# Two embedding tables move from gathers to one-hot products in the last batch, and the blocks between a tile's Gram chunks are set in another order

## The reference

```python
e = jnp.stack([tbl_0[ids[:, 0]], ..., tbl_25[ids[:, 25]]], axis=1)
combined = jnp.concatenate([e, r_dense_x[:, None, :]], axis=1)
interact = jnp.einsum('bfd,bgd->bfg', combined, combined)
z = interact[:, _TRIU_I, _TRIU_J]
h = jnp.concatenate([z.reshape(z.shape[0], -1), r_dense_x], axis=1)
h = jnp.maximum(h @ W_top1 + b_top1, 0.0)
h = jnp.maximum(h @ W_top2 + b_top2, 0.0)
y = h @ W_top3
```

## Time and profile before

| | |
|---|---|
| median of 3 runs | 385.13 us (384.95 to 386.6) |
| the profiled execution | 386.03 us, of which its span is 384.2 us |
| PE busy | 334.0 us, 87% |
| DVE, ACT, POOL busy | 61%, 49%, 70% |
| mean granted PE clock | 0.969 |

### The profile page before, as it was taken

One profiled execution on the slowest core, in us unless ns is written; L12 is line 12 of the kernel. 1 busy time (PEld: TensorE's weight loads), 2 busy tenths in 40 slices (PEclk: granted clock), 3 DMA queues, 4 the chain that ended last, 5 costly groups with the idle time before them and its releaser, 6 DMA issues.

```text
span 384.2 us, 12018 instructions
## 1 busy us (share of the span) xinstructions
PE 334.0 (87%) x5327; PEld 242.1 (63%) x5327; DVE 233.0 (61%) x389; ACT 186.9 (49%) x281; POOL 270.8 (70%) x288
## 2 busy tenths in 40 slices
PE   4999599778688989888998999988997899899776
PEld 3677477566576656557676666557676454578665
DVE  6889799687885829276896929467793011303030
ACT  6587634544515345345444434356444454655323
POOL 7777777777777777777777777777777777777100
PEclk9999989989989999989999999999999999989699
DMA  7998233433332423413343332423212221222000
GB/s 188 255 256 232 77 89 90 99 77 86 82 89 76 86 74 82 111 51 90 77 106 86 85 80 62 119 66 85 78 54 52 56 57 50 57 57 53 19 4 2
DMA packets 24195, 33.61 MB, mean 87 GB/s; under 512 B 6527, under 2 KB 17538, under 8 KB 24144
## 3 DMA queue, kind: packets, MB, share of 16 engines
q0 software_dynamic: 8960, 18.37, 18.2%
q1 hardware_dynamic: 15184, 14.48, 16.1%
HBM read 32.82 MB, written 0.01 MB: 85 GB/s over the span
## 4 chain that ended last, share of the span: by engine, by line
PE 54%; POOL 19%; issue 11%; DVE 7%; ACT 4%; DMA 3%; POOLq 0%; SPq 0%; DVEq 0%; ACTq 0%
POOL gat L372 19%; PE prod L431 12%; PE prod L433 11%; PE gram L460 8%; PE back L502 6%; PE front L405 5%; PE back L506 4%; DVE ring L708 4%; PE back L492 2%; ACT ct L600 1%; DVE ring L702 1%; DMA oh_last<-in_tbl,idx 1%; DMA gat<-in_tbl 1%; PE prod L417 1%; PE back L487 1%
## 5 line engine op out<-in xcount | busy, mean ns | idle before, releaser
L372 POOL DMA_INDIRECT gat<-in_tbl,idx x272 | 260.8, 959 | 83.0 <-issue 81.8
L708 DVE TENSOR_SCALAR ring<-idb,rowid 125x516 fp32r<-125x516 int32 x216 | 145.9, 741 | 16.9 <-PE prod L433 16.6
L431 PE MATMUL prod<-ring,tab_hi 125*128 125x512 f32 x264 | 110.0, 417 | 6.9 <-DVE ring L708 3.8
L433 PE MATMUL prod<-ring,tab_lo 125*128 125x512 f32 x264 | 106.1, 402 | 0.0
L600 ACT COPY ct<-front 128x512 f32<-128x512 f32 (+2 forms) x80 | 72.7, 964 | 25.0 <-PE front L405 22.6
L715 DVE COPY z<-gram 128x216 f32<-128x216 f32 x32 | 12.2, 382 | 111.1 <-PE gram L460 111.1
L460 PE MATMUL gram<-ct 128*32 128x27 f32 x4096 | 56.1, 196 | 17.1 <-issue 9.9
L460 PEld LDWEIGHTS gram<-ct 128*32 128x32 f32 x4096 | 46.7, 109 | 34.1 <-issue 24.8
L431 PEld LDWEIGHTS prod<-ring,tab_hi 125*128 125x128 f32 x264 | 51.4, 195 | 22.8 <-issue 8.4
L433 PEld LDWEIGHTS prod<-ring,tab_lo 125*128 125x128 f32 x264 | 51.2, 194 | 10.2
L405 PE MATMUL front<-ident,gat 128*128 128x128 f32 x272 | 42.7, 283 | 9.7 <-ACT ct L600 3.8
(11 more groups left out here) (73 smaller groups left out, 226.8 us busy)
## 6 DMA issues: line engine op xcount, KB each, us to landing
idb<-in_ids_t SPq DMA_DIRECT2D x27, 258.0 KB, 4.1
gat<-in_tbl,idx POOLq DMA_INDIRECT x272
oh<-in_tbl SPq DMA_DIRECT2D x3, 448.0 KB
oh<-in_dense_t SPq DMA_DIRECT2D x4, 256.0 KB, 3.1
gat<-in_tbl SPq DMA_DIRECT2D x2, 448.0 KB
h<-in_tbl SPq DMA_DIRECT2D x2, 448.0 KB
w1z<-in_w SPq DMA_DIRECT2D x1, 702.0 KB
w2s<-in_w SPq DMA_DIRECT2D x1, 512.0 KB
```

Source lines behind the costliest of these rows:

```text
L372: nc.gpsimd.indirect_dma_start(out=gat[:, t % GS, i, :], out_offset=None, in_=tables[GATHERED[i]][:, :], in_offset=bass.IndirectOffsetOnAx ...
L431: nc.tensor.matmul(prod[:, :], tab_hi[0:OH_P, m, k, :], ring[0:OH_P, k, 0:SB], start=(k == 0), stop=False)
L433: nc.tensor.matmul(prod[:, :], tab_lo[0:OH_P, m, k, :], ring[0:OH_P, k, 0:SB], start=False, stop=(k == OH_K - 1)).then_inc(used, 1)
L708: nc.vector.tensor_scalar(ring[0:OH_P, k, :], idb[0:OH_P, n % IDB, :, 0:IW], rowid[0:OH_P, k:k + 1], None, ALU.is_equal).then_inc(built, 1)
```

## The change

- Tables 7 and 10 (`LATE`, 1250 rows) are put last among the gathered columns. In tiles 12 to 15 they are not gathered: a tile has 15 gathered columns and four fills there. Their rows for the last batch are made by one-hot products in tile 12 (step `X`, ten chunks of 125 rows, 20 matmuls for a table). For this SP loads both tables to the unused half of `oh` late in batch 2, ACT splits off the high parts (step `V`, tile 11) and copies the rows to Gram banks (step `W`, tile 12), DVE subtracts for the low parts and builds the chunks, ACT copies the products (`copy_late_products`) and places them for each tile (step `Q`).
- In batches 0 to 2 a layer block or a one-hot field now stands between Gram chunks 1 and 2 of every tile; `H` is half a field.
- The first batch's extra gathers come with the first fill, not the last.
- In tile 15 and the tail the layer blocks and the pairs' transposes are put in another order, the second layer's matmuls go input by input, and the last two results are stored with one DMA.

```diff
+LATE = [7, 10]
+GATHERED = [f for f in range(26) if f not in ONEHOT + LATE] + LATE
+def fills_of(t):
+    return TF if t < LATE_T else (NG - NL + TCH - 1) // TCH
...
-        return T[0:1] + N[4:5] + T[1:2] + N[5:6] + T[2:3] + Z + T[3:4] + N[6:7] + E[0:4] + T[4:5] + G + E[4:7]
+        return T[0:1] + N[4:5] + T[1:2] + N[5:6] + Z + T[2:3] + N[6:7] + E[0:3] + T[3:] + E[3:4] + G + E[4:5]
     if last and u == 0:
-        return T[0:2] + J[0:0] + T[2:4] + Z + T[4:5] + J[0:2] + G[0:1] + PL + G[1:2] + J[2:3] + G[2:4]
+        return (X[0][0:1] + T[0:2] + X[0][1:] + T[2:3] + X[1][0:1] + Z + T[3:] + J[0:1] + X[1][1:] + [("Q", t)] + J[1:2]
+                + G[0:1] + PL + G[1:2] + J[2:3] + G[2:4])
...
     if u == 0:
-        return T[0:2] + O[0:1] + T[2:3] + Z + T[3:4] + J[0:1] + T[4:5] + O[1:2] + J[1:2] + G[0:1] + PL + G[1:4]
+        return T[0:2] + O[0:1] + T[2:3] + Z + T[3:4] + J[0:1] + T[4:5] + O[1:2] + G[0:1] + PL + G[1:2] + J[1:2] + G[2:4]
     if u == 1 and b == 0:
-        return T[0:2] + O[2:3] + T[2:3] + Z + T[3:4] + O[3:4] + T[4:5] + G[0:1] + PL + G[1:4]
+        return T[0:2] + O[2:3] + T[2:3] + Z + T[3:5] + halves(3, 0) + G[0:1] + PL + G[1:2] + halves(3, 1) + G[2:4]
     if u == 1:
-        return T[0:2] + J[2:3] + T[2:3] + O[2:3] + T[3:4] + J[3:4] + T[4:5] + Z + O[3:4] + G[0:1] + PL + G[1:4]
+        return T[0:2] + J[2:3] + T[2:3] + O[2:3] + T[3:5] + J[3:4] + Z + G[0:1] + PL + G[1:2] + O[3:4] + G[2:4]
...
-    return T[0:2] + J[5:6] + T[2:3] + O[6:7] + T[3:4] + Z + T[4:5] + O[7:8] + J[6:7] + O[8:9] + G[0:1] + PL + G[1:4]
+    if b == 0:
+        return T[0:3] + O[6:7] + T[3:4] + Z + O[7:8] + T[4:5] + halves(8, 0) + G[0:2] + halves(8, 1) + G[2:3] + PL + G[3:4]
+    return (T[0:2] + J[5:6] + T[2:3] + O[6:7] + T[3:4] + Z + T[4:5] + V[0:1] + O[7:8] + V[1:2] + J[6:7] + G[0:2] + O[8:9]
+            + G[2:3] + PL + G[3:4])
...
-END = [("Z", TILES - 1)]
+END = [("Z", TILES - 1), ("L", NB, 2, 1), ("L", NB, 3, 0)]
...
+            def load_late(x):
+                sp.wait_ge(placed, LATE_T)
+                src = tables[LATE[x]].rearrange("(p k) d -> p (k d)", k=LATE_K)
+                for lo, hi in ((0, OH_SPLIT), (OH_SPLIT, OH_P)):
+                    sp.dma_start(late_table(x)[lo:hi, :], src[lo:hi, :]).then_inc(late_in[x], 16)
...
+            def late_products(x):
+                bank_clear(("X", x))
+                pe.wait_ge(late_lo, x + 1)
+                for k in range(LATE_K):
+                    n = late_chunk(x, k)
+                    pe.wait_ge(built, n + 1)
+                    cols = slice(k * D, (k + 1) * D)
+                    nc.tensor.matmul(prod[:, :], late_high(x)[:, cols], ring[0:OH_P, n % OH_K, 0:SB],
+                                     start=(k == 0), stop=False)
+                    nc.tensor.matmul(prod[:, :], late_low(x)[:, cols], ring[0:OH_P, n % OH_K, 0:SB],
+                                     start=False, stop=(k == LATE_K - 1)).then_inc(used, 1)
...
+            def copy_late_rows(x):
+                if x == 0:
+                    act.wait_ge(gram_act, GC // 2 * LATE_T)
+                    act.wait_ge(gram_dve, GC // 2 * LATE_T)
+                else:
+                    act.wait_ge(late_lo, x)
+                for i, part in enumerate(late_parts):
+                    nc.scalar.copy(late_bank(i), late_table(x)[:, part]).then_inc(late_copied, 1)
...
+            def split_late(x):
+                dve.wait_ge(late_hi, x + 1)
+                for i, part in enumerate(late_parts):
+                    dve.wait_ge(late_copied, len(late_parts) * x + i + 1)
+                    ins = nc.vector.tensor_sub(late_low(x)[:, part], late_bank(i), late_high(x)[:, part])
+                ins.then_inc(late_lo, 1)
...
+                if t == LATE_T:
+                    split_late(0)
+                    for k in range(made, LATE_K):
+                        build_late(0, k)
                     pick_pairs(t - 1)
+                    split_late(1)
+                    for k in range(LATE_K):
+                        build_late(1, k)
```

More of the change, by code:

```diff
@@ L21 @@
 ONEHOT = [1, 5, 8, 12, 13, 14, 21, 24, 25]
-GATHERED = [f for f in range(26) if f not in ONEHOT]
+LATE = [7, 10]
+GATHERED = [f for f in range(26) if f not in ONEHOT + LATE] + LATE
 NG = len(GATHERED)
@@ L28 @@
 OH_SPLIT = 112
+NL = len(LATE)
+LATE_K = 10
+LATE_T = TILES - BT
 TCH = 4
@@ L78, in top1_row_order, with fill_number @@
     return rows + list(range(NPAIR, NPAIR + D))
+def fills_of(t):
+    return TF if t < LATE_T else (NG - NL + TCH - 1) // TCH
+def fill_number(t, c):
+    return sum(fills_of(i) for i in range(t)) + c
 def tile_steps(t):
@@ L86, in tile_steps @@
     last = b == NB - 1
-    T = [("T", t, c) for c in range(TF)]
+    T = [("T", t, c) for c in range(fills_of(t))]
     G = [("G", t, c) for c in range(GC)]
@@ L90, in tile_steps @@
     PL = [("P", t + 1)] if t + 1 < TILES else []
+    if LATE_T <= t < TILES - 1:
+        PL += [("Q", t + 1)]
+    X = [[("W", x), ("X", x)] for x in range(NL)]
+    V = [("V", x) for x in range(NL)] if t == LATE_T - 1 else []
     O = [("O", b + 1, m) for m in range(NO)]
@@ L162, with build @@
 NP = NO * NB - NX
-def build(nc, dense_t, ids, ids_t, w1, b1, w2, b2, w3, out, tables):
+def build(nc, dense_t, ids, ids_t, ids_late, w1, b1, w2, b2, w3, out, tables):
     with ExitStack() as ctx:
@@ L248, in build, with fill_columns @@
         y_out = sem("y_out")
-        def fill_columns(c):
-            return range(c * TCH, min((c + 1) * TCH, NG))
+        def fill_columns(t, c):
+            part = (c + TF - 1) % TF if t < BT else c
+            return range(part * TCH, min((part + 1) * TCH, NG if t < LATE_T else NG - NL))
         def extra(t, c):
-            return NX if t < BT and c == TF - 1 else 0
+            return NX if t < BT and c == 0 else 0
         def extra_rows(t, e):
@@ L260, in gathers_landed @@
         def gathers_landed(t, c):
-            return sum(len(fill_columns(c)) + extra(i, c) for i in range(t % GS, t + 1, GS))
+            return sum(len(fill_columns(i, c)) + extra(i, c) for i in range(t % GS, t + 1, GS))
         def raw_table(m):
@@ L375, in gather @@
                         ).then_inc(gathered[t % GS][c], 16)
[L376 to L377 removed]
+                    for e, f in enumerate(ONEHOT[NA:NA + extra(t, c)]):
                         nc.gpsimd.indirect_dma_start(
@@ L426, in onehot_products @@
                     pe.wait_ge(lo_ready, m + 1)
-                if n > 0:
+                if n > 0 and chunks[0] == 0:
                     pe.wait_ge(prod_free, n)
-                for k in range(OH_K):
+                for k in chunks:
                     pe.wait_ge(built, OH_K * n + k + 1)
@@ L765, in _ @@
                         copy_gram(t, c)
-                    if ahead_of(t)[c]:
-                        build(onehots_of(t + 1)[0], made, made + ahead_of(t)[c])
+                    for k in range(made, made + ahead_of(t)[c]):
+                        following = onehots_of(t + 1)[0]
+                        if following[0] == "X":
+                            build_late(following[1], k)
+                        else:
+                            build_chunk(following[1], following[2], k)
                     made += ahead_of(t)[c]
```

183 lines of the change are left out of this document (138 added, 45 removed).

## The result

The change made the kernel slower. Its median is 390.7 us (390.47 to 391.74, four runs), where the kernel before took 385.6 us on the same chip (384.95 to 386.6, four runs). The ratio is 1.012, with a 95% interval of 1.008 to 1.016. The profiled execution took 391.7 us, with a span of 389.9 us against 384.2 before. I had forecast 382.0 us in a range up to 386.4, faster with a chance of 0.67: wrong in its sign, and outside its range.

What follows compares the result with a forecast made beforehand. PE was taken to bound the kernel before the last batch and the gathers at the end. The terms -10.0 + 15.4 - 1.1 - 7.4 gave -3.1 us, so 382.0 from the 385.13 median, range 378.3 to 386.4.

Steps and rivals of the forecast that it cites:

- So before the last batch PE is the slower of the two, and at the end the gathers set the time.: Whole kernel: PE is 8.3 us behind the gathers in tile 11, but waits 1.98 us for one in tile 15.
- Gram chunks apart: 3.6 us for four.: Tiles 3 to 11: splitting four chunks two and two takes 3.6 us, gaining 7.3 us for tiles 4 to 9.
- rival 3: Gram chunks of tiles 3 to 9: the "issue" gap is supply and returns behind the block; 389.6 us, chance 0.12.
- Tile 12 starts at 286.1, 10.0 earlier.: Upstream of tile 12: PE gains from split chunks until the gathers limit it at tile 11's last fill, 273.9.
- Tile 12: +15.4.: Tile 12: product matmuls and waits for ACT and DVE put its first Gram chunk at +27.3, 15.4 us later.
- Tiles 13 and 14: 33.9.: Tiles 13 and 14: they lose their fifth fill and a 0.57 us wait, taking 33.9 us instead of 35.0.
- Tile 15 and tail: 26.6.: Tile 15 to the end: without a gather wait, half-clock blocks and fifth fill, 26.6 us where it was 33.96.
- The slower rival: Same as rival 3: the gap returns, tile 12 starts at 293.7, less than 4.9 us earlier; 389.6 us, chance 0.12.
- The second rival: Tiles 12 and 15: more half clock, both tile 12 waits bringing a full stretch; 383.3 to 386 us, chance 0.21.
- tile 12 starting after 290: Start of tile 12: a sign that the forecast is wrong; the forecast had it near 286.
- pairs of chunks over 2.3 us: Gram chunks in tiles 4 to 11: a sign of being wrong; the forecast had 1.7 to 1.9 us each pair.
- PE waits for a gather in tile 10 or 11: Tiles 10 and 11: listed as a sign that the forecast is right, PE having caught up with the gathers.

Runs made afterwards that it cites:

- m2: Kernel before with only tile 15, the tail and the place of the first batch's extra gathers as in the changed kernel, all tables gathered: 380.03 us, ratio 0.985.
- g1: Changed kernel without late tables: all 17 tables gathered in every tile, new order of batches 0 to 2 and new tail kept; 379.62 us, ratio 0.985.
- m1: g1 with SP's load of the next batch's dense rows issued two places later: 380.76 us, ratio 0.986.
- m3: Changed kernel with g3's shorter chain, the dense load two places later, and late tables' loads held until tile 11's third fill is turned: 387.73 us, ratio 1.004.
- g3: Changed kernel with ACT's order around tile 12 edited, late rows copied ahead of placing columns and of the first table's products: 387.52 us, ratio 1.001.
- f1: Changed kernel with SP's load of the next batch's dense rows issued two places later: 391.88 us, ratio 1.011.
- f2: Changed kernel with tiles 5 and 9 put back in the order of before, Gram chunks together: 391.42 us, ratio 1.013.
- g2: Late tables and new tail as in the changed kernel, batches 0 to 2 in the order of before: 394.33 us, ratio 1.021.

## Why the prediction was wrong

The span came out 8.8 us over the sum (389.9 against 381.1): 4.4 at the start of tile 12, 1.2 in tile 12, 3.1 in tile 15 and the tail, 0.1 between.

**"So before the last batch PE is the slower of the two, and at the end the gathers set the time."** Right for the kernel before. In m2 PE turns the last column 0.7 us and in g1 0.3 us after it can have landed, so without late tables PE can't gain more than that by working faster upstream: g1, m1 and m2 are 379.6, 380.8 and 380.0, with three different upstreams. What followed from it, "Both must get shorter for the time to fall much", was wrong: in m2 the gathers are as long as before, only tile 15 and the tail are shorter, and the time falls by 1.5%.

**Gram chunks apart: 3.6 us for four.** Right: 3.5 to 3.9 in tiles 4 and 6 to 11. Outside tile 5, rival 3's gap did not come back behind the block; the total of 6.8 us from tile 6 to tile 12 is even more than the 5.3 I had for tiles 7, 8, 9 and 11 (3 x 1.2 + 1.7).

**"Tile 12 starts at 286.1, 10.0 earlier."** This step failed, by 4.4 us, and all of it ahead of tile 6. I had counted gains of 1.5, 1.1 and 2.6 us in tiles 3, 4 and 5 and taken the gathers as a limit in tile 11 only. In fact PE is on the gather stream already in tiles 3 and 4 and gives back 7.9 us there in four waits (2.00, 1.68, 1.59 and 2.61), where before had one of 2.46. The gathers come at the same pace as before: the fourth fill of tile 4 could be turned from about 124.5 on, and before PE was there at 126.91.

Then comes the 4.0 us stop in tile 5. PE comes to the place behind record 1851 at 156.77, where before it came at 162.45, 5.7 us later; the packet with its next instructions starts at 158.5, where before it started at 160.9, only 2.4 later. The moved layer block, with only the pairs' transposes between, stands right ahead of the Gram chunks and releases SP's dense load and an ids load (514 KB) at 153.8. Their packets run from 154.8 to 158.7, so the instruction packet starts just as they end. It does so within 0.3 us in eleven of the thirteen profiles from the fast chips, the kernel before among them (161.0 and 160.9). In m1 and m3, where the dense load is moved, the ids load (258 KB) is there alone; it ends at 156.9 and 157.5, the packet starts at 157.1 and 157.4, and stops of 2.39 and 1.85 us remain, about 2 us less than in their counterparts g1 (4.30) and g3 (4.05). The two other profiles are f1 and f2, without a stop, where the packet had started at 148.0 and 149.6. Why it came so early in these two, and why in the others it did not come in the time without SP's loads ahead of them (149.7 to 154.8 in the changed kernel), no run shows. What I had called a gain of 2.6 us was a loss: tile 5 takes 27.6 us (141.13 to 168.70), where before it took 23.8.

Taking the stop away is worth nothing here, which I had not seen either: in f1 and f2 the earlier PE waits for gathers slowed by the late tables' loads, and m3 shows the wait following the loads. The prediction said that "the only thing queued behind them on SP is the late ids". That was the wrong queue to look at: what stands in line with 1.28 MB of loads are the gathers of POOL, on the same DMA engines.

**Tile 12: +15.4.** The chain was laid out rightly. The first late product came at +4.5 (4.3 predicted) after 3.40 us idle (3.4), the third fill at +10.7 (10.6), the layer block at +14.25 (14.1), with 2.31 us idle before it. Only the half clock was mis-sized: I had counted half of a second stretch and it came in full, and the first Gram chunk is at +28.5, not +27.3. The page quoted from the Trainium skill ("TensorE: Matmul & The Clock Gate", section "HAM oscillation — how this bites in real kernels") said that each pause is paid for again. The pauses of its example are longer than the 2.31 us here; here both were paid, so far the trace agrees. A wait of 0.94 in the same place (g3) was not, so not each pause is. g3 also shows that part of this was ACT's order alone: with five copies moved the tile is 4.2 us shorter.

**Tiles 13 and 14: 33.9.** Right to 0.1 us.

**Tile 15 and tail: 26.6.** Right as a count of the work: m2 has 26.8. In the changed kernel it is 29.7, as the Gram chunks there stop twice for instructions, 3.1 us together. In the kernels with late tables and the new tail the stops there are 2.1 to 3.7 us together; in those without late tables (g1, m1, m2) 1.5 to 2.3, mostly behind the Gram chunks, and before it was 1.35 behind them, where I had kept it inside the old 9.06. The late tables' 32 matmuls more move the place behind record 5256 from the second layer into the Gram chunks, where PE comes to it sooner; the nine profiles with late tables have the longer stops there in all but one (2.07, f2) against the three without. How long each stop gets is not explained.

**What it adds up to.** By medians: the tail is worth -1.5% (m2), the order of batches 0 to 2 nothing on top of that (g1), the late tables +2.7% on top of both (1.012 / 0.985), 10 to 11 us; with the old order below them they cost 3.6% (g2 against m2, 1.021 / 0.985). They take away eight gathers, 10 us of POOL's time, from a stream that after the new tail holds PE up by nothing in its last tile, and they put 12.6 us more on PE in tile 12 (35.8 against g1's 23.2): 9.4 of products, and waits of 5.7, where g1 has one of 2.1, with half clock for 6.8 us in all behind them in both. My error in kind was to count on an earlier end of the gathers, from 356.2 to 346.2. The last one started at 350.20, as POOL now waited for PE, and PE turned its column 19.6 us later: PE never came near that end, while what the late tables put on PE came in full.

The slower rival was right in its condition, that the gap is a matter of supply, as the packets show, but not in what follows: the gap came back only in tile 5 and tile 15, not behind every block, and tile 12 started at 290.49, not 293.7. By its own test (less than 4.9 us earlier; it was 5.6) it did not come. Its price, 389.6, is near the result by chance. The second rival's two full half-clock stretches are what happened in tile 12. Of the signs that I had listed as wrong ones, "tile 12 starting after 290" came true by 0.5 us and "pairs of chunks over 2.3 us" in tile 5 (6.12); "PE waits for a gather in tile 10 or 11" did not come.

## What to carry to other kernels

When work is moved from one engine to a second, ask whether the second can use the time that the first gives back: here the gathers ceased to hold anybody up once the last tile's blocks stood ahead of its last fill, and that rearrangement alone was the faster kernel (380 us). Price a bulk load by the gathers (here 7.3 us instead of 2.6) and, as it seems, by the instruction fetches (some 2 us in tile 5) that share the DMA engines with it, not by its own queue; and when a step is moved, look at which semaphore it raises and which transfer that lets go. Where two engines hand over a chain, order the copies so that those that the waiting engine needs come first: that was worth 3 us of 390.

## What the runs showed of the hardware that was not expected

- PE's instructions come by DMA, in packets of 16 KB on a queue of their own, 42 in each profile, which is one for about 127 matmul records (5359 or 5327 in all). The Trainium skill ("Runtime: NRT & Kernel Launch", section "Instruction fetch mechanics") has these blocks of 16 KB, and calls the cost of crossing from one to the next mostly hidden; in this trace it is hidden only while PE is slow in using them up. They were never closer than 3.4 us, and after a stop PE went on 2.3 to 2.7 us after a packet's start (158.5 to 160.79; 370.7 to 373.33; 374.5 to 376.78). Four Gram chunks, 256 records, run in 2.4 us, so they use up what two packets bring in less time than lies between two packets. Rows of the DMA view of the changed kernel, for 157 to 158.4 us and for 158.4 to 161 us (queue, kind, packets, MB, share of 16 engines); q1 carries SP's loads, q0 the gathers:

```profile
q1 hardware_dynamic: 222, 0.15, 51.2%
q0 software_dynamic: 2, 0.01, 1.7%
```

```profile
q0 software_dynamic: 126, 0.25, 30.2%
q1 hardware_dynamic: 42, 0.02, 3.1%
q8 instruction: 1, 0.02, 2.2%
```

- An indirect gather of 128 rows of 512 bytes that lands in 2.6 us on quiet DMA engines landed in 5.9 and 7.3 us beside 1.28 MB of table loads, while POOL went on issuing every 1.25 us and showed nothing of it.
- After idle times of 2.11, 2.31, 2.61 and 3.40 us in the changed kernel the clock read 0.50 for 3.3 to 3.4 us, and after one of 4.02 us for 6.8 us. The length of the idle time does not decide it: one of 2.14 us in g1 and one of 1.31 us in m1's tile 14 were followed by 6.8 us at 0.50, those of 2.00 and 1.68 us in tile 3 of the changed kernel by none (1.00 from 93 to 123), and after one of 0.94 us (g3) it stayed at full speed.
